# Five attention stages without their loop, with norm, key and query work, transfers and masking in a new order

## The reference

```python
h = layernorm(x)
q, k, v = h @ Wq.T + bq, src @ Wk.T + bk, src @ Wv.T + bv   # src: h or the context
logits = einsum('bqhd,bkhd->bhqk', heads(q), heads(k)) * scale (+ mask)
x = x + einsum('bhqk,bkhd->bqhd', softmax(logits), heads(v)).reshape(...) @ Wo.T + bo
```

## Time and profile before

| | us |
|---|---|
| three runs | 4828.27, 4782.36, 4789.26 (median 4789.26) |
| the profiled execution | 4813.37 |
| its span | 4811.6 |
| mean granted clock in it | 0.928 of 2.4 GHz |

### The profile page before, as it was taken

One profiled execution on the slowest core, in us unless ns is written; L12 is line 12 of the kernel. 1 busy time (PEld: TensorE's weight loads), 2 busy tenths in 40 slices (PEclk: granted clock), 3 DMA queues, 4 the chain that ended last, 5 costly groups with the idle time before them and its releaser, 6 DMA issues. The chain is left out here.

```text
span 4811.6 us, 76408 instructions
## 1 busy us (share of the span) xinstructions
PE 4392.0 (91%) x22610; PEld 2202.8 (46%) x22610; DVE 2706.3 (56%) x6114; ACT 2289.0 (48%) x4789; POOL 1240.8 (26%) x1277
## 2 busy tenths in 40 slices
PE   5999999889896889899999999999899799999998
PEld 3555543333464333334444443333366455555555
DVE  3555677776102777787766767777400344444443
ACT  2444456555221556554444446665422355454553
POOL 1111111111221111111111111111022566666664
PEclk9888899998797889999999999998799899999999
DMA  4433434333001443433222223434100000000000
GB/s 106 64 55 59 69 73 77 66 62 59 16 0 23 89 73 62 72 58 63 47 46 46 43 47 77 81 61 74 33 16 0 27 5 10 10 10 10 10 6 10
DMA packets 115381, 218.33 MB, mean 45 GB/s; under 512 B 22320, under 2 KB 25008, under 8 KB 113328
## 3 DMA queue, kind: packets, MB, share of 16 engines
q1 hardware_dynamic: 114992, 213.79, 24.2%
HBM read 39.11 MB, written 4.19 MB: 9 GB/s over the span
## 5 line engine op out<-in xcount | busy, mean ns | idle before, releaser
L907 ACT ACTIVATE Pr<-ST 128x512 f32<-128x512 f32 (+3 forms) x2560 | 1359.1, 564 | 1370.8 <-PE ST L492 1069.9
L1089 DVE TENSOR_REDUCE mx<-MX 128x1 f32<-128x512 f32 (+3 forms) x1408 | 855.0, 629 | 503.8 <-PE MX L492 468.2
L492 PE MATMUL ST<-stk 50*128 50x512 f32 (+3 forms) x2560 | 1115.5, 486 | 16.5 <-ACT Pr L907 13.9
L492 PE MATMUL MX<-stk 48*128 48x512 f32 (+3 forms) x1760 | 773.5, 475 | 165.1 <-DMA stk<-lo 87.4
L492 PE MATMUL OV<-Pr,V 128*32 128x512 f32 (+3 forms) x5120 | 710.4, 630 | 1.5 <-ACT Pr L907 1.5
L492 PEld LDWEIGHTS MX<-stk 48*128 48x128 f32 x1760 | 329.3, 199 | 781.1 <-DVE mx L1089 414.2
L1408 POOL TENSOR_SCALAR Pr<-Pr,mx 128x128 f32<-128x128 f32 (+3 forms) x512 | 548.4, 1083 | 385.4 <-DVE mx L1227 385.4
L492 PEld LDWEIGHTS ST<-stk 50*128 50x128 f32 x2560 | 461.1, 199 | 139.7 <-ACT Pr L907 108.9
L1089 DVE TENSOR_REDUCE mx<-OV 128x1 f32<-128x512 f32 (+3 forms) x640 | 399.9, 625 | 136.3 <-PE OV L492 135.9
L1342 POOL CAST mhl<-mx 128x16 fp32r<-128x16 f32 x160 | 31.9, 199 | 1464.3 <-DVE mx L1089 1110.0
L1339 POOL TENSOR_TENSOR X<-X,brow 128x1024 f32 (+1 forms) x56 | 132.3, 2363 | 1014.7 <-DVE X L1041 1014.7
(11 more groups left out here) (134 smaller groups left out, 6766.7 us busy)
## 6 DMA issues: line engine op xcount, KB each, us to landing
stk<-hi SPq DMA_DIRECT2D x640, 128.0 KB, 3.9
stk<-lo SPq DMA_DIRECT2D x320, 128.0 KB, 4.0
misc<-misc SPq DMA_DIRECT2D x160, 128.0 KB, 3.8
sums<-misc SPq DMA_DIRECT2D x160, 128.0 KB, 4.0
misc<-in_ctx_t SPq DMA_DIRECT2D x24, 512.0 KB, 4.9
W_even<-in_w SPq DMA_DIRECT2D x4, 1024.0 KB, 5.6
W_even<-in_w SPq DMA_DIRECT2D x2, 2048.0 KB, 7.8
XH<-in_ctx_rows SPq DMA_DIRECT2D x8, 512.0 KB, 4.2
```

What stands on the lines that cost most here:

```text
L492: return nc.tensor.matmul(o, l, r, start=start, stop=stop)
L907: nc.scalar.activation(Pr[:, i % 2, h, q0:S], ST[h % 2][:, q0:S], ACT.Exp).then_inc(ex_done, 1)
L1089: nc.vector.tensor_reduce(m, bank[:, 0:k_n], AX.X, ALU.max).then_inc(mx_red, 1)
```

## The change

1. The loop is gone: all slots are written out with constant targets.
2. Order of jobs. Turned rows go from (2,3), (3,3) to (0,2), (1,2) of even slots. Keys and queries go to (2,2), (3,2) and (4,2), (5,2) in even slots, and to (0,2), (1,2) and (2,2), (3,2) in odd ones; values go to the steps 4 to 7 of odd slots, one job a step. high_part and low_part follow. The turn of the next unit's maxima goes from (4,2) to (5,2).
3. The norm (statistics, combine, GpSimd's three parts) is done one slot ahead, in the odd slot. The second half of the output is added at (0,1) of the next odd slot, and the bias with it.
4. Sums: one row per head is moved (few, 64 runs of 32 elements), one reciprocal of 128x32 is taken at (1,3) instead of four of 128x128 from (3,1) on, and two transfers spread it through DRAM to 128 rows (spread_rows, widen).
5. SyncE: keys' stack, then move, then queries' stack, then the next row of maxima, instead of both rows of maxima, both stacks, and then move.
6. SELF0: no mask products. VectorE adds the mask while it takes the maxima; GpSimd clears the upper triangle of the exponentials (clear), and values waits for that (cleared) and stands at j = 3 instead of 1.

```diff
-            with eng.Fori(0, 3) as k:
-                for n in range(4):
-                    slot(4 * k + (2 + n), (2 + n) % 4, 2 * k + (1 + n // 2), k + 1, stages(2 + n))
...
@@ SyncE, slot @@
-                    if on["m"]:
-                        max_rows(U + 1, 1 - half, 0)
-                    if on["a"]:
-                        stack(U + 2, half, 0, GB + 1)
-                    if on["b"]:
-                        move(U, half, 0, GB)
+                        spread_rows(U - 1, 1 - half)
+                    if on["b"]:
+                        max_rows(U, half, 1)
+                    if on["tail"]:
+                        widen(U - 1, 1 - half)
...
+                    if on["a"]:
+                        stack(U + 2, half, 0, GB + 1, 0)
+                    if on["b"]:
+                        move(U, half, 0, GB)
+                    if on["a"]:
+                        stack(U + 2, half, 0, GB + 1, 1)
+                    if on["m"]:
+                        max_rows(U + 1, 1 - half, 0)
...
+                def spread_rows(U, half):
+
+                    sp.wait_ge(recip_done, U + 1)
+                    sp.dma_start(spread[half].rearrange("h (c n) -> (h c) n", n=32), few[:, half, :]).then_inc(spread_out, 16)
+
+                def widen(U, half):
+                    waits(sp, (spread_out, 16 * (U + 1)), (at_ready, BASE + U))
+                    rows = spread[half].rearrange("h (a n) -> h a n", a=1).broadcast_to([2 * G, HD, S])
+                    sp.dma_start(sums[:, half, :], rows).then_inc(spread_in, 16)
@@ TensorE, slot @@
-                            if j == 1 and on["b"] and i > 0:
+                            if j == (3 if ATTN[s][1] else 1) and on["b"] and i > 0:
                                 values(ATTN[s][1], U, half, par, i - 1)
...
-                                if half == 0 and at in ((2, 3), (3, 3)):
+                                if half == 0 and at in ((0, 2), (1, 2)):
...
-                                if half == 1 and at in ((0, 2), (0, 3), (1, 2), (1, 3)):
-                                    project_values(GB1, wq(sa, 2), source, i, j - 2)
+                                if half == 1 and i >= 4 and j == 2:
+                                    project_values(GB1, wq(sa, 2), source, (i - 4) // 2, i % 2)
...
-                    if causal:
-                        last = add_later(ST[h % 2][:, q0:q0 + P], lo_p, C_MK)
@@ VectorE @@
+                    elif causal:
+                        k_n = P * (qt + 1)
+                        nc.vector.tensor_tensor_reduce(bank[:, 0:k_n], bank[:, 0:k_n], later0[:, S - k_n:S], 1.0, -3.0e38,
+                                                       ALU.add, ALU.max, m).then_inc(mx_red, 1)
...
-                    part = sums[:, half, P * j:P * j + P]
-                    nc.vector.reciprocal(part, part).then_inc(recip_done, 1)
+                    for g in range(2):
+                        dve.wait_ge(ov_moved[g], 32 * U)
+                    nc.vector.reciprocal(few[:, half, :], few[:, half, :]).then_inc(recip_done, 1)
@@ GpSimd @@
+                def clear(U, i):
+
+                    waits(pool, (ex_done, 4 * (8 * U + i + 1)), apart=True)
+                    q0 = P * (i % 4)
+                    tile = Pr[:, i % 2, :, q0:q0 + P]
+                    nc.gpsimd.affine_select(tile, tile, [[0, G], [1, P]], ALU.is_ge, 0.0, 0, -1).then_inc(cleared, 1)
```

More of the change, by code:

```diff
@@ L251, in run_slots @@
                     on.update(tail=True, op=True)
[L252 to L258 removed]
+                if s + 1 in JOINED and u >= UNITS - 2:
                     on.update(a=True, m=True)
@@ L381, in slot @@
                     half, U, GB = c % 2, UNITS * n + u, NB * n + b
-                    if isinstance(u, int) and u == 1:
+                    if u == 2:
                         load_next(s)
[L384 to L387, removed]
                     if on["stack1"]:
-                        stack(U + 1, 1 - half, 1, GB + half)
+                        for kind in range(2):
+                            stack(U + 1, 1 - half, 1, GB + half, kind)
@@ new lines, in slot @@
+                            if at == (1, 0) and norm is not None:
+                                combine(NB * sn + bn)
+                            if at == (1, 3) and on["tail"]:
+                                invert(U, 1 - half)
+                            if at in (((4, 1), (6, 1)) if half == 0 else ((2, 2), (4, 1))) and on["a"]:
+                                low_part(sa, U, half, (i - 4) // 2 if half == 0 else (i - 2) // 2)
+                            if half == 0 and on["op"] and at == (7, 1):
+                                output_sum(se, be, GB, 0)
@@ L1348, in attention @@
                 n = ATTN_NO[s]
+                causal = ATTN[s][1]
                 def slot(u, c, b, p, on):
@@ L1352, in slot @@
                     U, GB = UNITS * n + u, NB * n + b
+                    norm = norm_of(s, u)
+                    if norm is not None:
+                        N, rows = NB * norm[0] + norm[1], xt(norm[1], 0, NT)
+                    clears = causal and on["b"]
+                    if on["tail"] and ATTN[s - 1 if u == 0 else s][1]:
+                        clear(U - 1, 7)
                     if on["b"]:
                         maxima(U, half, 1)
-                    if half == 0 and on["a"]:
-                        sa, ba = a_of(s, u, b)
-                        layer_norm(NB * sa + ba, xt(ba, 0, NT), la_full, JOBS * GB + 2)
+                    if clears:
+                        clear(U, 0)
@@ L1358, in slot @@
+                    if norm is not None:
+                        rows_scale(N)
+                    if clears:
+                        clear(U, 1)
+                    if norm is not None:
+                        rows_centre(N, rows, la_full, JOBS * (GB + u % 2) + 2)
+                    if clears:
+                        clear(U, 2)
+                    if norm is not None:
+                        rows_times(N)
+                    if clears:
+                        clear(U, 3)
                     if on["m"]:
```

173 lines of the change are left out of this document (89 added, 84 removed).

## The result

The changed kernel takes 4974.4 us (median of four runs, 4963.2 to 4979.7), the kernel before in the same batch 4785.8. The ratio is 1.035, interval 1.031 to 1.040: slower by 3.5%. The forecast was 4814 with a range up to 4900, so both fell. The profiled execution took 4963.2 us, 11 under its median, where that of the kernel before lay some 27 over its own.

A forecast was written before the change was run, and what follows sets the result against it. TensorE, busy 91% of the span, was taken as the bound. Gains of some 375 us were to be given back by SyncE's queue stalls, total +25: 4838 us profiled, 4814 median, range 4660 to 4900 for 8 in 10.

The forecast's parts named there:

- What bounds the kernel: Whole kernel: TensorE, busy 91% of the span, no other engine over 56%; five attention stages take 3004 of 4812 us.
- part 4: SyncE's queue: move waits for the output projection, idling TensorE 7.0 us at 36 odd slots, 252 us, plus low clock.
- slower by the clock: Rival, chance 0.20: cross slots bound by TensorE alone lose half of each low us behind a stall; 4872 us.
- Part 5: SELF0 without mask products: 8.3 us off TensorE's 29.5 a slot; exponential waits give back 4.8, clears cost odd slots 1.7.
- give-back of 4.8 us a slot: SELF0: values after both blocks make the second block's scores wait for exponentials, 0.6 us x 8.
- forecast without stalls: Stage sums before the queue stalls: SELF0 8 x 57, CROSS0 450, CROSS1 and CROSS2 480 each, SELF2 750 us.
- slower by GpSimd: Rival, chance 0.12: a clear in SELF0 costs 3 us and comes late in each step, +80 us; 4894 us.
- Part 3: Reciprocals: four of 0.94 us a slot become one of 0.3; VectorE loses 3.4 us, spreading transfers hidden except at stage ends.
- first rival: Late query stacks don't bind, so the queue stalls and their low clock go: 4411 us, chance 0.08.
- Part 6: SELF2 is TensorE's alone: 93.8 us a pair, nothing hides the new stall; stage 842 us, +71.
- the loop: Written out, it loses 7.66 us stalls at two branches in CROSS0 and CROSS1, smaller ones elsewhere; counted in stage sums.
- The sum: Stage changes -30, -14, -12, +71, +2 and ends +8: total +25 us, 4838 profiled, 4814 median.

The follow-up runs named there:

- leanest kernel: Also "best version": changed kernel with move behind queries' stack and row of maxima, SELF0's values at j = 1, reciprocal at (2,3); 4474.8 us, ratio 0.933.

## Why the prediction was wrong, step by step

**What bounds the kernel, and part 4: right.** 36 gaps of 7.45 us (forecast 7.0) at the places named, for the reason named; 10.4 us each with their low clock where nothing else waits, 374 in all, against the forecast's 403. On top of the idle that is 2.9 us a gap on average, where the forecast had 3.5 to 6. By stage (move first less move last in the leanest kernel, 356 us in the five windows of the profiled executions) the cross stages' gaps cost 3.0 on top, SELF2's 2.2 (forecast 4.5), SELF0's 1.2 (forecast 6). SELF0's price depends on what else waits there: with values late it was 7.6 (648 less 543 us over seven gaps).

The forecast took its low time, 10.7 us a gap, from one stall. The same length of window behind the other three stalls of over 7 us at its branches has clocks of 0.50, 0.57 and 0.78, and behind the 36 gaps of the changed kernel the mean is 0.66, from 0.50 to 0.84. One of the milder ones:

```profile
821.30:832.00 10.70, 10.70 (x48) 3.48 (x52) 8.61 (x20) 5.76 (x11) 3.16 (x3) 0.75 0.46 61
```

That is 7.3 low us a gap and not 10.7. So the rival "slower by the clock" did not come true, but its half us for a low us was about right. In CROSS0 of the leanest kernel with the move first, the mean behind the seven gaps is 0.71, 3.1 us a gap at half speed, and 3.2 were measured on top of the idle; in SELF2 it is 2.9 for 2.2 measured. The Trainium skill's rule behind that rival (TensorE: Matmul & The Clock Gate, Terms), low time times the missing share of the clock, fits CROSS0's trace and is somewhat too high in SELF2.

**Part 5: the step that failed.** "0.66 x 320/512 = 0.41" scaled a block by its mean width, and the 8.3 us that this took off TensorE's 29.5 a slot were booked as 8.3 us of time. Maxima and scores run side by side, the wider sets the block, and so a block without mask products takes 0.66 us on average by the forecast's own formula, (25.0 - 9.1 - 5.3)/16. The products' removal took 4.5 us off a slot's TensorE, not 8.3: 3.8 us a slot, 60 us a stage. Nor did the 4.5 turn into time: SELF0 without products and with clears was only 24 us shorter (478 for 502), 1.5 us a slot, at a granted clock of 0.91 instead of 0.97 and with 33 us of TensorE idle instead of 15. Forecast, the products less the delay by the clears, were 8.3 x 16 - 1.7 x 8 = 119 us.

The give-back of 4.8 us a slot for the exponentials was about right: 4.1 in the best version, 5.4 in the changed kernel (635 to 548 us, 16 slots). So removing the products and moving the values, taken together, was a loss: the kernel with the products and with values between the blocks took 4520.0 us, the one without products and with values late 4553.0.

This accounts for SELF0's miss. With the move last, the reciprocal later and values late, the stage took 543 us, where the forecast without stalls has 456: 87 us, 95 from the products and 12 the other way from the give-back, with 4 left over. The gaps (106 us for 91) and the early reciprocal, with which the stage is 14 us shorter beside the gaps, cancel. Why the lighter stage runs at a lower clock was not taken apart.

The Trainium skill (GPSIMD Engine Reference, Elementwise — side-by-side cycle accounting) was the better guide for the clear: its 769 ns against 638 measured, and 1270 to 1563 from the rows that I took. The rival "slower by GpSimd" falls with it: 22 us of waits in SELF0.

**Part 3: right in size, wrong in place.** One reciprocal of 0.35 us, and CROSS0's slots without stalls came out as forecast, but only once it stood a step later. Priced at 1.0 us in SELF0's even slots alone, at (1,3) it costs 156 to 181 us as soon as the 7.45 us gap no longer covers it. Beside the gap it costs 25 to 36 at most. The forecast's first rival (4411, no late stacks) carried that omission: with the move last and the rest unchanged, the time was 4709.

**Part 6 and the loop: right.** SELF2 took 833 us for 842; without the gap 751 for 750. For the loop the forecast had named no sum of its own; written out alone it is worth 31 us.

**The sum.** By profiled executions the forecast was 125 us short: SELF0 88, the cross stages 46, less 9 in SELF2. The other 35 of the 160 between 4814 and 4974 is where the two profiled executions lay to their medians: 24 over for the first (by the three runs shown), 11 under for the other. In the cross stages the gaps cost what was forecast (219 us for 220, move first less move last). What the forecast lacked there is some 34 us that remain in the best version (CROSS0 454 for 450, CROSS1 500 and CROSS2 490 for 480 each) and some 15 of the early reciprocal. The 34 were not taken apart. The gains were there and were given back: written out, reordered and with leaner VectorE work this kernel runs in 4475 us, and three placements (a move ahead of transfers that TensorE waits for, a reciprocal ahead of its data, values behind the second block) take 500 us of it.

## What to carry to other kernels

In an in-order DMA queue, a transfer that waits for the end of a slot belongs behind every transfer that the start of the next slot needs; the same holds for an instruction at the head of an in-order engine, which must stand where its data has surely come. Price two streams that share TensorE block by block with the wider of the two, never with a mean width, and do not book work taken off the busiest engine as time. Take the low clock behind a gap from several gaps, not from one. A cost that a larger stall covers comes back when that stall is taken away, so measure placements in combination before judging one of them.

## What was not expected of the hardware

The clock falls behind short gaps too: behind 1.75 and 1.34 us of idle, with half a us of work between them, a cross slot ran at 0.66 of full clock over ten us, while a 7.45 us gap was followed by 0.54 over 10.7 us (behind 891.8) or only 0.75 (behind 821.3). In the kernel with the early reciprocal the slot is 5.0 us longer (35.0 for 30.0), of which 3.1 are TensorE's busy time for the same work (31.9 for 28.8): the idle that one sees in the waits is the smaller part. The windows of that slot and of the stretch behind the long gap:

```profile
711.40:746.40 35.00, 31.90 (x162) 11.64 (x160) 24.90 (x46) 20.60 (x39) 9.44 (x10) 0.90 0.36 69
```

```profile
891.80:902.50 10.70, 10.69 (x36) 3.21 (x36) 6.71 (x17) 4.39 (x9) 2.47 (x3) 0.54 0.44 58
```

And a small transfer (2x4x512) took 2.5 us from its issue to TensorE's restart when no stack transfers stood just ahead of it in the queue, 4.3 us behind three of 128 KB.
